# Loading the first weights inside the one block of a two-layer decoder kernel, with head rows picked over 128 rows and a new table of turns

## The chip, the cores and the metric

The kernel runs on one core of one Trainium2 chip. The metric is the device time of one execution in microseconds; lower is better. A time quoted for a kernel is the median of its executions.

## What is computed

The input is x of 8 rows of the batch, 256 positions each, 512 features, and a context of 8 x 256 x 128. Two layers follow, each with a LayerNorm ahead of every part and a residual sum behind it:

```
x = x + attn(ln(x), Wq, bq, Wk, bk, Wv, bv, Wo, bo)   # layer 0: 16 heads, causal
x = x + xattn(ln(x), ctx, ctx)                        # 32 query heads, 8 key heads
x = x + ffn(ln(x), w_gate, w_up, w_down)              # operands rounded to a block format
x = x + ssm(ln(x), Wx, Wg, bg, Wo, A, Dp)             # layer 1: recurrence over 256 steps
x = x + xattn2(ln(x), ctx, Wq, Wkv_expand, Wout)      # 16 heads, causal
x = x + experts(ln(x), W, gate_w, A, B)               # top 2 of 8 low-rank experts
```

The recurrence needs `softplus(delta[h] + B[n])` for 32 heads h and 128 states n. The kernel builds that sum in a bank of PSUM: it adds to the B part the row of `delta` that belongs to head h, spread over all 128 partitions.

## The kernel before

A row is one element of the batch (256 x 512, f32, tile `XR`, five buffers). Each part of a layer is a class (`Attention`, `Mixing`, `Quantised` and `Hidden` for layer 0; `States`, `Attention` again as `cross`, and `Experts` for layer 1). For each engine a part has a generator that yields between steps. `side_by_side` takes a string of letters per engine, the table `TURNS0`; each letter advances one generator by one step. So the order of the instructions on each engine is written out by that table, and the engines meet only at semaphores. All eight rows run through layer 0 and then through layer 1, with neighbouring rows and parts interleaved.

Products of f32 values are made of three f16 products: a weight is split into a high part (a copy by ACT, L271) and a low part (a subtraction by DVE, L277). `Loader` does this for a list of weights, with three staging buffers: the DMA into a staging buffer waits until the low part of the item three places earlier is made.

Ahead of the main block the program has two small blocks.

- In the first (L212) POOL makes the constants `ident`, `ident16`, `identh`, `hide_qk`, `minus_half` and `ones_of_four`.
- In the second (L1774) SP and ACT issue the loads of Wq, Wk, Wv, Wo, bv and of the biases, and ACT and DVE split them. `ffn_room` stages them. A clearing of semaphores with a barrier over all engines follows (`clear`, L180).
- The main block then begins. On POOL it starts with `attn.pool_setup` (L383 to L387: clears `attn_NM` and fills 32 partitions of `attn_stack` twice) and `mix.pool_setup` (L835 to L840 in `mix_V` and `mix_K`), ahead of all turns.

In the main block the first row goes this way. SP loads it (L1802). DVE takes its moments (L323 to L329), POOL the inverse root (L333, L335), ACT scales it (L341), TensorE transposes it (L402), ACT and DVE split the transpose (L555, L607). TensorE multiplies by Wq and Wk (L194 for all such products), ACT and DVE split the result into `attn_P` (L569, L619). SP sends this to `attn_stack` (L694), DVE takes the maxima of the scores (L630, L634) and splits them (L639), and SP sends them on (L700). Then ACT makes the exponentials (L587), POOL masks them (L677), TensorE multiplies by V (L499, L507), and DVE takes the reciprocal of the sums (L643), once per row.

Beside this, `Quantised` rounds the 12 chunks of the ffn weights, 1 MB each: a load into one of two raw buffers in `ffn_room` (L729), and ten DVE steps (L738 to L768), of which four of 128 x 2048 take 2.3 us and two take 1.2 us, and the maximum (L738) 2.3 us.

In layer 1 `States.pe` picks a head's row (L1321): the stationary operand is one column of `pickh` [64, 32], repeated 128 times, the moving operand `ssm_db` [64, 256], in which partitions 0 to 31 hold the high and 32 to 63 the low part of `delta`. There are 256 of these matmuls.

## Time and profile before

| | us |
|---|---|
| median of 3 executions | 1780.51 |
| lowest and highest | 1776.14, 1786.61 |
| the profiled execution | 1775.17 |
| its span, first to last instruction | 1773.4 |
| TensorE, VectorE, ScalarE, GpSimd busy | 1442.2, 1373.2, 1057.3, 429.4 |
| mean granted clock of TensorE | 0.906 of 2.4 GHz |

The profile is that of the one profiled execution. A share of busy time is a mean over stages. PE is TensorE, DVE VectorE, ACT ScalarE, POOL GpSimd, SP the engine that issues most DMAs; SPq is its queue. By the chain that ended last TensorE has 39% of the span, VectorE 29%, ScalarE 16%, issue 9% and GpSimd 3%.

### The profile page before, as it was taken

The page shows a single profiled execution, that of the slowest core. Times are in us where ns is not written, and L with a number is a line of the kernel's source. Part 1 is how long each engine was busy: PE and PEld are TensorE (multiplying, and loading weights), DVE is VectorE, ACT ScalarE, POOL GpSimd, SP SyncE. Part 2 cuts the span into 40 slices and gives each one's busy share as a digit, 9 for nine tenths or more (in the row PEclk, how much of TensorE's full clock was granted, in tenths as well). Part 3 has the DMA queues.
Part 4 walks back from the last instruction along what each step waited for, and adds up shares of the span by engine and source line. Part 5 has one row for each costly group of instructions (what it writes and reads, how often), then busy time and mean ns, then how long its engine had stood idle before and what let it go on. Part 6 is the DMA issues. An engine that isn't in the chain of part 4 may idle for free.

```text
span 1773.4 us, 30964 instructions
## 1 busy us (share of the span) xinstructions
PE 1442.2 (81%) x11863; PEld 725.5 (41%) x11920; DVE 1373.2 (77%) x2111; ACT 1057.3 (60%) x1878; POOL 429.4 (24%) x486
## 2 busy tenths in 40 slices
PE   0767877878988888879878766889998899998986
PEld 0443543344443443444333422345444445454542
DVE  3989998899598796885887897858676877868743
ACT  2242642563743735646566757688869698987531
POOL 4241322151230512311331231212221213030310
PEclk9787978899999999999988987798989899899988
DMA  6302130202002002002210003101010101101010
GB/s 226 87 27 61 55 96 24 67 14 43 26 13 67 13 29 40 26 8 61 76 49 25 25 0 111 40 1 40 25 40 18 47 15 50 37 16 40 13 49 24
DMA packets 92082, 76.38 MB, mean 43 GB/s; under 512 B 9376, under 2 KB 73888, under 8 KB 91424
## 3 DMA queue, kind: packets, MB, share of 16 engines
q1 hardware_dynamic: 91504, 74.14, 15.1%
q8 instruction: 96, 1.57, 0.4%
q14 instruction: 50, 0.41, 0.1%
q10 hardware_dynamic: 432, 0.27, 0.1%
HBM read 39.24 MB, written 9.44 MB: 27 GB/s over the span
## 4 chain that ended last, share of the span: by engine, by line
PE 39%; DVE 29%; ACT 16%; issue 9%; POOL 3%; SPq 1%; DMA 1%; ACTq 0%; DVEq 0%; POOLq 0%
PE bank L194 10%; DVE mix_NM L1025 5%; PE bank L938 3%; PE bank L1125 3%; PE bank L499 3%; PE bank L459 3%; DVE ssm_HS L1485 2%; ACT ssm_DA L1433 2%; PE bank L507 2%; PE bank L487 2%; PE bank L923 2%; DVE ffn_m L1079 2%; PE bank L461 2%; ACT ssm_DD L1436 2%; DVE ffn_Z L1089 1%
## 5 line engine op out<-in xcount | busy, mean ns | idle before, releaser
L998 ACT ACTIVATE mix_P<-bank 128x512 f32<-128x512 f32 x256 | 140.6, 600 | 76.8 <-PE bank L923 75.4
L1485 DVE TENSOR_TENSOR_SCAN ssm_HS<-ssm_DA,ssm_DD 128x1024 f32<-128x1024 f32 x64 | 151.7, 2371 | 31.8 <-ACT ssm_DD L1436 27.2
L1025 DVE TENSOR_REDUCE mix_NM<-bank 128x2 f32<-128x512 f32 x256 | 163.9, 682 | 15.3 <-PE bank L898 14.9
L677 POOL TENSOR_SCALAR_AFFINE_SELECT cross_P<-cross_P 128x256 f32<-128x256 f32 x128 | 90.0, 711 | 331.5 <-ACT cross_P L587 331.4
L677 POOL TENSOR_SCALAR_AFFINE_SELECT attn_P<-attn_P 128x256 f32<-128x256 f32 x128 | 98.6, 782 | 225.1 <-ACT attn_P L587 224.9
L1243 POOL TENSOR_TENSOR ffn_room<-ffn_room 128x512 f32<-128x512 f32 x64 | 87.9, 1373 | 224.0 <-DVE ffn_room L1207 122.9
L1433 ACT ACTIVATE ssm_DA<-ssm_Z,A_T 128x255 f32<-128x255 f32 x256 | 112.6, 503 | 4.5 <-DVE ssm_HS L1485 4.0
L587 ACT ACTIVATE attn_P<-bank 128x384 f32<-128x384 f32 x128 | 63.4, 496 | 66.1 <-PE bank L488 65.7
L587 ACT ACTIVATE cross_P<-bank 128x384 f32<-128x384 f32 x128 | 62.7, 490 | 55.8 <-PE bank L488 55.3
L938 PE MATMUL bank<-mix_P,mix_V 128*32 128x256 f32 x1024 | 74.3, 416 | 11.7 <-DVE mix_XN L1041 11.6
L1125 PE MATMUL bank<-gate,ffn_XQ 128*128 128x512 bf16 x227 | 64.0, 399 | 24.0 <-DVE ffn_room L1207 19.2
L1207 DVE SCALAR_TENSOR_TENSOR ffn_room<-ffn_room,bank 128x512 f32<-128x512 f32 x64 | 43.4, 679 | 50.2 <-ACT ffn_room L1178 50.1
L923 PE MATMUL bank<-mix_Q,mix_K 64*128 64x256 f16 x512 | 53.2, 286 | 35.4 <-ACT mix_P L998 19.3
L1491 DVE TENSOR_TENSOR ssm_HS<-ssm_HS,ssm_CS 128x1024 f32<-128x1024 f32 x64 | 78.7, 1230 | 1.0
L1408 ACT ACTIVATE ssm_Z<-bank 128x512 f32<-128x512 f32 x128 | 71.6, 596 | 10.2 <-PE bank L1321 9.6
L898 PE MATMUL bank<-mix_K,mix_Q 64*128 64x256 f16 x512 | 53.1, 286 | 28.3 <-DVE mix_NM L1025 24.7
L1125 PE MATMUL bank<-up,ffn_XQ 128*128 128x512 bf16 x247 | 70.5, 410 | 1.7 <-issue 1.0
L1436 ACT ACTIVATE ssm_DD<-ssm_Z 128x1024 f32<-128x1024 f32 x64 | 67.6, 1056 | 0.0
L1178 ACT ACTIVATE ffn_room<-bank 128x512 f32<-128x512 f32 x64 | 38.2, 598 | 46.0 <-PE bank L1125 45.9
L1151 PE MATMUL bank<-down,ffn_room 128*128 128x512 bf16 x237 | 61.9, 393 | 1.6 <-issue 0.8
L487 PE MATMUL bank<-attn_stack 128*128 128x256 f16 x128 | 39.2, 306 | 27.6 <-ACT attn_P L587 21.3
L1321 PE MATMUL bank<-ssm_db,pickh 64*128 64x256 f16 x256 | 49.4, 296 | 14.7 <-ACT ssm_Z L1408 13.7
(403 smaller groups left out, 4141.3 us busy)
## 6 DMA issues: line engine op xcount, KB each, us to landing
attn_stack<-attn_P SPq DMA_DIRECT2D x64, 128.0 KB, 2.5
cross_stack<-cross_P SPq DMA_DIRECT2D x64, 128.0 KB, 2.5
XR<-x SPq DMA_DIRECT2D x8, 512.0 KB, 4.6
ffn_room<-f_gate SPq DMA_DIRECT2D x4, 1024.0 KB, 7.7
attn_stack<-attn_P SPq DMA_DIRECT2D x64, 64.0 KB, 2.1
ffn_room<-f_up SPq DMA_DIRECT2D x4, 1024.0 KB, 5.2
ffn_room<-f_down SPq DMA_DIRECT2D x4, 1024.0 KB, 4.9
x_mid<-XR SPq DMA_DIRECT2D x8, 512.0 KB, 3.0
```

Source lines behind the costliest of these rows:

```text
L194: last = nc.tensor.matmul(out, a_, b_, start=(start and i == 0), stop=(stop and i == len(terms) - 1))
L587: nc.scalar.activation(self.p[h % 8][:, :], bank[self.b[0]][:, 0:S + P], ACT.Exp, scale=HD1 ** -0.5).then_inc(self.p_ready, 1)
L677: nc.gpsimd.affine_select(out=diagonal, in_=diagonal, compare_op=ALU.is_ge, fill=0.0, base=0, pattern=[[0, 2], [1, P]], channel_multiplier ...
L923: last = nc.tensor.matmul(bank[b4[i]][:, k * S:(k + 1) * S], self.k[rows, v // 2, k * P:(k + 1) * P], self.q[rows, v, :], start=(k == 0), ...
L938: last = nc.tensor.matmul(bank[b][32 * j:32 * j + 32, half * S:(half + 1) * S], self.v[:, k, g, :], self.p[(4 * g + j) % 8][:, k * S:(k + ...
L998: nc.scalar.activation(self.p[h % 8], bank[b4[h % 2]][:, :], ACT.Exp, scale=HD2 ** -0.5).then_inc(s["p_ready"], 1)
L1025: nc.vector.tensor_reduce(self.nm[:, t, 16 * i + 2 * g:16 * i + 2 * g + 2], bank[b4[u % 3]][:, :].rearrange("p (c k) -> p c k", c=2), AX.X ...
L1125: last = nc.tensor.matmul(bank[b][:, :], self.xq[:, k, T * P:(T + 1) * P], w[:, k, fb * 512:(fb + 1) * 512], start=(k == 0), stop=(k == DC ...
L1243: nc.gpsimd.tensor_tensor(self.inter[q % 2][:, 512 * (g % 2):512 * (g % 2) + 512], self.sg[g % 2], self.up[g % 2], ALU.mult).then_inc(s["i ...
L1433: nc.scalar.activation(self.da[:, G % 2, k, 1:S], self.z[:, h, 1:S], ACT.Exp, scale=self.A_T[:, h:h + 1])
L1436: nc.scalar.activation(self.dd[:, G % 2, :, :], self.z[:, HG * g:HG * g + HG, :], ACT.Square).then_inc(s["da_ready"], 1)
L1485: nc.vector.tensor_tensor_scan(flat(self.hs), flat(self.da), flat(self.dd), 0.0, ALU.mult, ALU.add).then_inc(s["hs_ready"], 1)
```

## The change

The two small blocks are gone. What they did is now in the main block.

- SP gets two more streams, the weights and the biases. Their staging is now `attn_stack` (two halves) and the front of `attn_P`, no longer `ffn_room`. bv comes ahead of Wo.
- ACT and DVE get one more stream each, for the splitting.
- POOL makes the constants first. `attn.pool_setup` and `mix.pool_setup` become streams with turns of their own; the first waits until all five weights are split.
- TensorE waits for the constants once, for the low parts of Wq and Wk ahead of the first product, for the fourth item (bv) ahead of the first V, for all ahead of the first product with Wo. ACT waits for all five and for the biases ahead of its first split of q and k (which writes where Wv was staged), and SP ahead of the first DMAs into `attn_stack`. POOL waits for the biases ahead of adding bo.
- Loaders that share semaphores count on from the items before (`first`, `used`), since nothing is cleared between them.
- `pickh` and `ssm_db` are 128 partitions high; partitions 64 to 127 of `ssm_db` are set to 0 once, on POOL, in place of a second writing of one column. The pick is a matmul over 128 rows.
- The table of turns is another one for all engines.

```diff
             def sp(self, sp, i, free=None):
...
                 if i >= n:
-                    sp.wait_ge(self.low_ready, i - n + 1)
+                    sp.wait_ge(self.low_ready, self.first + i - n + 1)
...
-                        if n == B:
-                            pe.wait_ge(weights_f.low_ready, len(weights_f.items))
+                        if n == self.first:
+                            pe.wait_ge(*self.weights.ready(2))
...
+                    if n == self.first and t == 0 and self.bv is not None:
+                        pe.wait_ge(*self.weights.ready(4))
...
-                    if n == B and c == 0:
-                        act.wait_ge(weights_f.low_ready, len(weights_f.items))
+                    if n == self.first and c == 0:
+                        act.wait_ge(*self.weights.ready())
+                        if self.bq is not None:
+                            act.wait_ge(small_in, 48)
...
-                        last = nc.tensor.matmul(bank[b][:, i * S:(i + 1) * S], self.pickh[:, 2 * u + i:2 * u + i + 1].broadcast_to([2 * NH, P]),
+                        last = nc.tensor.matmul(bank[b][:, i * S:(i + 1) * S], self.pickh[:, 2 * u + i:2 * u + i + 1].broadcast_to([P, P]),
...
-            weights_0 = Loader("l0w", [(whole(w), chunk(A[n])) for w, n in ((wq, "Wq"), (wk, "Wk"), (wv, "Wv"), (wo, "Wo"))]
-                               + [(whole(bv), A["bv"].partition_broadcast(P))],
-                               [room[:, 2048 * i:2048 * i + 2048] for i in range(3)])
+            weights_0 = Loader("l0w", [(whole(w), chunk(A[n])) for w, n in ((wq, "Wq"), (wk, "Wk"), (wv, "Wv"))]
+                               + [(whole(bv), A["bv"].partition_broadcast(P)), (whole(wo), chunk(A["Wo"]))],
+                               [attn.stack[:, i, :, :].rearrange("p h k -> p (h k)").bitcast(F32) for i in range(2)]
+                               + [attn.space[:, 0:2048]])
...
-            pickh = sb(l1, "pickh", [2 * NH, NH], F16)
+            pickh = sb(l1, "pickh", [P, NH], F16)
...
-            db = sb(l1, "ssm_db", [2 * NH, S], F16)
+            db = sb(l1, "ssm_db", [P, S], F16)
...
-        clear([r.num for r in weights_0.loaded + [weights_0.high_ready, weights_0.low_ready, small_in, done_pool]])
...
+        def clear_attention(pool, n):
+            yield
+            pool.wait_ge(*weights_0.ready())
+            attn.pool_setup(pool)
+
+        def clear_mixing(pool, n):
+            yield
+            mix.pool_setup(pool)
...
+                             in_turn(lambda i: weights_0.sp(sp, i), items_0),
+                             in_turn(lambda n: load_biases(sp, n), 1),
...
                 own = Own(pool, done_pool)
-                attn.pool_setup(pool)
-                mix.pool_setup(pool)
-                side_by_side(TURNS0["pool"], in_turn(lambda n: attn.norm.pool(pool, own, n)),
+                make_constants(own)
+                side_by_side(TURNS0["pool"], in_turn(lambda n: clear_attention(pool, n), 1),
+                             in_turn(lambda n: clear_mixing(pool, n), 1),
+                             in_turn(lambda n: attn.norm.pool(pool, own, n)),
```

A line or two of the table of turns, SP's:

```diff
-        "caaaaaeeccbebeeebbcceeebbcceeccbebccbccbdaccbccdabccdabccccbdccbccbdcckkkffjkkkccdfcdfllldgflllg"
+        "eacleaaakkkackkebcbeeebbeebccbeeccebccbeccbccbdaccbdaccbccdabccbccdccbccbdccjmmfmfmmmccdfcdfnnnd"
```

How the instructions of three queues stand now. First SP, from the start of the main block of the changed kernel (`f_gate` are chunks of the ffn weights, `ctx_cols` and `ctx_rows` the context, `a_...` the weights and biases of the first attention, `x` the rows):

```order
L739 DMA ffn_room<-f_gate 128x4x512
L1804 DMA XR<-x 128x2x512
L857 DMA mix_CF<-ctx_cols 128x256
L861 DMA mix_VR<-ctx_rows 128x128 x2
L1789 DMA l_bq<-a_bq 128x4
L1789 DMA l_bk<-a_bk 128x4
L1789 DMA l_bo<-a_bo 128x512
L739 DMA ffn_room<-f_gate 128x4x512
L1804 DMA XR<-x 128x2x512 x3
L266 DMA attn_stack<-a_Wq 128x4x512
L266 DMA attn_stack<-a_Wk 128x4x512
L266 DMA attn_P<-a_Wv 128x4x512
```

Before, SP had the four weights and bv in a block of their own, and then the context, five rows and two chunks; now a chunk, row 0, the context, the biases, the second chunk and rows 1 to 3 stand ahead of Wq.

DVE before, in the main block behind its first instruction (L738 to L750 are the rounding of chunk 0, L607 the low part of the transposed first row):

```order
L323 BN_STATS attn_stats<-XR 128x6 x2
L326 BN_AGGR attn_mv<-attn_stats 128x2 x2
L328 TENSOR_SCALAR attn_negative<-attn_mv 128x2
L329 TENSOR_SCALAR attn_var<-attn_mv 128x2
L738 TENSOR_REDUCE w_max<-ffn_room 128x64
L607 TENSOR_TENSOR attn_XL<-bank,attn_XH 128x4x128 x2
L323 BN_STATS attn_stats<-XR 128x6 x2
L326 BN_AGGR attn_mv<-attn_stats 128x2 x2
L328 TENSOR_SCALAR attn_negative<-attn_mv 128x2
```

DVE of the changed kernel, from the maximum of chunk 0 on (L278 makes a low part, L615 is the former L607, L748 to L778 the former L738 to L768):

```order
L748 TENSOR_REDUCE w_max<-ffn_room 128x64
L751 TENSOR_SCALAR w_max<-w_max 128x64
L753 TENSOR_SCALAR w_e<-w_max 128x64
L755 TENSOR_SCALAR w_inv<-w_e 128x64
L757 TENSOR_SCALAR w_sc<-w_e 128x64
L760 TENSOR_TENSOR ffn_room<-ffn_room,w_inv 128x2048
L278 TENSOR_TENSOR l_wq_l<-attn_stack,l_wq_h 128x2048
L278 TENSOR_TENSOR l_wk_l<-attn_stack,l_wk_h 128x2048
L278 TENSOR_TENSOR l_wv_l<-attn_P,l_wv_h 128x2048
```

and, after the low parts of Wk, Wv and bv and the moments of row 1:

```order
L330 TENSOR_SCALAR attn_var<-attn_mv 128x2
L615 TENSOR_TENSOR attn_XL<-bank,attn_XH 128x4x128 x2
L763 TENSOR_SCALAR ffn_room<-ffn_room 128x2048
L766 TENSOR_SCALAR ffn_room<-ffn_room 128x2048
L769 SCALAR_TENSOR_TENSOR ffn_room<-ffn_room 128x2048
L278 TENSOR_TENSOR l_wo_l<-attn_stack,l_wo_h 128x2048
L772 TENSOR_TENSOR ffn_room<-ffn_room 128x2048
L627 SCALAR_TENSOR_TENSOR attn_P<-bank,l_bq,attn_P 128x256
```

Before, all five low parts stood in front of everything, and only the chunk's maximum stood ahead of the low part of the transposed row. Now five steps of chunk 0 and four low parts do, and the low part of Wo stands behind three more steps of the chunk and ahead of the first split of q (L627).

POOL before, at the start of the main block (`attn_NM` and `attn_stack` are cleared and filled by `attn.pool_setup`, `mix_V` and `mix_K` by `mix.pool_setup`):

```order
L383 MEMSET attn_NM 128x64
L385 MEMSET attn_stack 32x4096
L387 MEMSET attn_stack 32x4096
L835 MEMSET mix_V 128x512
L838 MEMSET mix_K 32x2048 x2
L840 MEMSET mix_V 128x16
L1050 MEMSET mix_P 128x64x16
L333 ISA
L333 TENSOR_TENSOR attn_rstd<-attn_var,minus_half 128x2
L335 TENSOR_TENSOR attn_shift<-attn_negative,attn_rstd 128x2
L671 TENSOR_TENSOR XR<-XR,l_bo 128x1024
```

POOL of the changed kernel, after the constants:

```order
L1060 MEMSET mix_P 128x64x16
L334 TENSOR_TENSOR attn_rstd<-attn_var,minus_half 128x2
L336 TENSOR_TENSOR attn_shift<-attn_negative,attn_rstd 128x2
L681 TENSOR_TENSOR XR<-XR,l_bo 128x1024
L334 TENSOR_TENSOR attn_rstd<-attn_var,minus_half 128x2
L336 TENSOR_TENSOR attn_shift<-attn_negative,attn_rstd 128x2
L385 MEMSET attn_NM 128x64
L387 MEMSET attn_stack 32x4096
L389 MEMSET attn_stack 32x4096
L845 MEMSET mix_V 128x512
L848 MEMSET mix_K 32x2048 x2
L850 MEMSET mix_V 128x16
```

Before, `attn_NM`, both fills of `attn_stack`, `mix_V` and `mix_K` stood ahead of the first inverse root; now only the clearing of `mix_P` does, and they stand behind the roots of rows 0 and 1; the first mask (L687) follows them.

## Rows read from the trace of the kernel before

**Rows 1.** The page: busy time, and 40 slices of the span (tenths)

```profile
PE 1442.2 (81%) x11863; PEld 725.5 (41%) x11920; DVE 1373.2 (77%) x2111; ACT 1057.3 (60%) x1878; POOL 429.4 (24%) x486
...
DVE  3989998899598796885887897858676877868743
...
PEclk9787978899999999999988987798989899899988
```

**Rows 2.** Windows: length; PE, PEld, DVE, ACT, POOL busy (count); clock, DMA share, GB/s

```profile
0.00:25.00 25.00, 0.00 (x0) 0.00 (x0) 9.77 (x5) 9.49 (x6) 2.36 (x19) 1.00 0.56 189
25.00:50.00 25.00, 9.01 (x58) 7.25 (x59) 12.34 (x24) 3.94 (x7) 18.32 (x13) 1.00 0.64 221
```

**Rows 3.** Timeline of the opening: start, duration, engine, line, operation, idle before

```profile
3.58 0.43 SPq L265 DMA_DIRECT2D ffn_room<-a_Wq  x1
...
9.80 1.90 ACT L271 CAST l_wq_h<-ffn_room 128x2048 f16<-128x2048 f32 x1 [3.35 <-DMA ffn_room<-a_Wq]
11.73 2.29 DVE L277 TENSOR_TENSOR l_wq_l<-ffn_room,l_wq_h 128x2048 f16<-128x2048 f32 x1 [11.73 <-ACT l_wq_h L271]
...
23.36 0.69 DVE L277 TENSOR_TENSOR l_bv_l<-ffn_room,l_bv_h 128x512 f16<-128x512 f32 x1
25.02 0.34 SPq L847 DMA_DIRECT2D mix_CF<-ctx_cols  x1
...
25.23 3.51 POOL L385 MEMSET attn_stack<- 32x4096 f16 x1
...
26.35 2.48 SPq L1802 DMA_DIRECT2D XR<-x  x5
...
32.95 3.65 POOL L838 MEMSET mix_K<- 32x2048 f16 x2
...
37.70 0.71 POOL L333 TENSOR_TENSOR attn_rstd<-attn_var,minus_half 128x2 f32<-128x2 f32 x1
...
38.72 1.52 ACT L341 ACTIVATE attn_XN<-XR,attn_shift,attn_rstd 128x512 f32<-128x512 f32 x2 [11.26 <-POOL attn_shift L335]
39.05 2.29 DVE L738 TENSOR_REDUCE w_max<-ffn_room 128x64 f32<-128x2048 f32 x1 [6.71 <-DMA ffn_room<-f_gate]
...
42.21 0.69 DVE L607 TENSOR_TENSOR attn_XL<-bank,attn_XH 128x512 f16<-128x512 f32 x1 [0.16 <-ACT attn_XH L555]
...
42.96 0.40 PE L194 MATMUL bank<-attn_XH,l_wq_h 128*128 128x256 f16 x1 [1.40 <-DVE attn_XL L607]
```

**Rows 4.** Timeline of the first row's attention, DVE

```profile
48.34 0.48 DVE L619 SCALAR_TENSOR_TENSOR attn_P<-bank,l_bq,attn_P 128x256 f16<-128x256 f32 x1 [0.81 <-ACT attn_P L569]
...
49.13 1.22 DVE L753 TENSOR_SCALAR ffn_room<-ffn_room 128x2048 int32<-128x2048 int32 x1
...
57.49 0.47 DVE L619 SCALAR_TENSOR_TENSOR attn_P<-bank,l_bq,attn_P 128x256 f16<-128x256 f32 x1
...
103.66 1.76 DVE L643 RECIPROCAL attn_RC<-bank 128x256 f32<-128x256 f32 x1 [3.76 <-PE bank L507]
```

**Rows 5.** The same timeline, ACT: the first exponential

```profile
79.61 0.49 ACT L587 ACTIVATE attn_P<-bank 128x384 f32<-128x384 f32 x1 [3.68 <-PE bank L488]
```

**Rows 6.** Windows in which the DMA engines are full

```profile
9.80:16.50 6.70, 0.00 (x0) 0.00 (x0) 3.01 (x2) 3.79 (x2) 0.00 (x0) 1.00 0.98 339
28.00:41.00 13.00, 1.41 (x7) 1.42 (x8) 4.04 (x7) 1.78 (x3) 10.96 (x10) 1.00 1.01 363
```

**Rows 7.** Line L1321, the picks: duration ns min/median/max, first and last start

```profile
L1321 PE MATMUL bank<-ssm_db,pickh x256: 267/269/418, 929.6 to 1638.1; 64*128 64x256 f16 x128
```

**Rows 8.** The page's group for the picks: busy, mean ns, idle before, releaser

```profile
L1321 PE MATMUL bank<-ssm_db,pickh 64*128 64x256 f16 x256 | 49.4, 296 | 14.7 <-ACT ssm_Z L1408 13.7
```

**Rows 9.** Window of low clock in the second half, all engines

```profile
1301.00:1305.00 4.00, 4.00 (x15) 1.01 (x13) 3.33 (x5) 0.00 (x0) 0.00 (x0) 0.50 0.69 149
```

**Rows 10.** TensorE groups by shape in that window

```profile
L459 PE MATMUL bank<-cross_P 32*128 32x256 f16 x10 | 3.0, 402 | 0.0
```

**Rows 11.** Line L643 in the second half: one reciprocal closes each row's attention

```profile
L643 DVE RECIPROCAL cross_RC<-bank x8: 1756/1758/1759, 1179.6 to 1728.9; 128x256 f32<-128x256 f32 x8
```

More of the change, by code:

```diff
@@ L247, in __init__, with ready @@
                     self.loaded, self.high_ready, self.low_ready = before.loaded, before.high_ready, before.low_ready
+                self.first = 0 if before is None else len(before.items)
+                self.used = [0 if before is None else len(range(i, len(before.items), len(stage))) for i in range(len(stage))]
+            def ready(self, count=None):
+                return self.low_ready, self.first + (len(self.items) if count is None else count)
             def staged(self, i):
@@ L357, in __init__ @@
                 self.qk = self.space[:, 0:2 * DC * S].bitcast(F16).rearrange("p (i c k) -> p i c k", i=4, c=DC)
-                self.rest = 3 if before is None else 6
+                self.rest, self.first = (3, 0) if before is None else (6, B)
+                self.weights = weights
                 for_sems = lambda part: sem(f"{name}_{part}") if before is None else before.signals[part]
@@ L534, in pe @@
                         b = self.b[(2 + t) % 3]
+                        if n == self.first and c == 0 and t == 0 and self.bv is not None:
+                            pe.wait_ge(*self.weights.ready())
                         if c == 0:
@@ L682, in sp @@
                 sp.wait_ge(self.qk_ready, DC * n + DC)
-                if n == B:
-                    sp.wait_ge(weights_f.low_ready, len(weights_f.items))
+                if n == self.first:
+                    sp.wait_ge(*self.weights.ready())
                 if n:
```

212 lines of the change are left out of this document (101 added, 111 removed).

## The prediction

> **What bounds the kernel now.** I read the page first. TensorE is busy for 81% of the span and VectorE for 77%, so neither is full everywhere; the slices show DVE at 9 tenths from the third slice on, and low only in the first two [rows 1]. So the opening is the place to look, and I went on to windows. In the first 25 us DVE works 9.77 us, ACT 9.49 and TensorE not at all; in the next 25 TensorE works 9.01 and DVE 12.34 [rows 2]. DVE is thus idle for 27.9 of the first 50 us, in a stretch behind which it is the busiest engine.
>
> The timeline of the opening gives the chain [rows 3]. The first weight is asked for at 3.58, behind the block of constants, and lands by 9.80. The last low part (bv) starts at 23.36 and ends at 24.05; the first DMA of the main block is issued at 25.02. Then POOL clears: `attn_stack` from 25.23, 3.51 us and as long again, `mix_K` until 36.60. Its first inverse root comes only at 37.70, and ACT, which scales row 0 at 38.72, had been idle for 11.26 us for it. DVE waits 6.71 us for chunk 0 and has its maximum at 39.05. The low part of row 0 starts last at 42.21, and the first product with Wq at 42.96. From there DVE leads: its first split of q starts at 48.34, the last at 57.49 [rows 4], the first exponential at 79.61 [rows 5], the reciprocal at 103.66 [rows 4].
>
> **The change part by part.** *Start of the DMAs.* SP has no work in the block of constants, so its first issue moves from 3.58 to about 0.8, where POOL's first constant is written in this trace (an estimate). The barrier, the clearing of semaphores and the second start go too, 0.97 us from 24.05 to 25.02 [rows 3].
>
> *Landing of the weights.* They now queue behind other bytes: two chunks (2.10 MB), rows 0 to 3 (2.10), context (0.26), bo (0.26). Wq, Wk and Wv add 1.05 MB each. With the DMA engines full they moved 363 GB/s over 13 us, and 339 among the weights alone [rows 6]. I take 363, since the mixture of chunks and rows is that of that window. The first weight took 2 us before bytes flowed, so they flow from 2.8. Wq has 5.77 MB up to its end: 18.7. Wk lands at 21.6, Wv at 24.5. With 339 Wv lands at 26.0. The Trainium skill (DMA: Bandwidth & Descriptors, section "Where 436 GB/s comes from") puts the limit of HBM for one core at about 358 GB/s; by it Wv would land at 24.8, and the trace's 363 stands just above it.
>
> *Split of the weights.* ACT needs 1.90 us and DVE 2.29 us for one of 128 x 2048 [rows 3]. While waiting, DVE does row 0's moments, the maximum of chunk 0 and its first multiplication, 2.29 each; all that is over by about 16.5. Low parts then end at 18.7 + 1.90 + 2.29 = 22.9 (Wq), 25.8 (Wk), 28.7 (Wv), 29.4 (bv, 0.69). The moments of row 1 take 1.8 (1.29 at L323 and three short ones), the two low parts of the transposed row 1.4. So the first product with Wq starts at **32.6**, against 42.96: 10.4 us sooner, and chunk 0 is one multiplication further.
>
> *First split of q.* ACT may write where Wv was staged only after all five splits. Wo is issued once Wk is split (25.8), lands at about 30 behind row 4 and bv, and is cast by 32. DVE comes to it after three steps of the chunk (1.22, 1.23 and 2.28, the durations of [rows 4]): 32.6 + 4.7 + 2.3 = 39.6. ACT then needs 0.94, DVE one more long step (41.9), and the four pairs of L627 with one long step between end at about 48, against 58.4. That is again 10.4, and DVE has then done the whole of chunk 0, one long step more than before.
>
> *The rest of row 0's attention.* The steps are the same and DVE has the same rounding to do up to the reciprocal (three chunks in both). SP's 16 DMAs to `attn_stack` follow the split of q, and the six for `mix_K`, formerly early, stand behind them, ahead of the maxima; they end before the maxima are split, so they cost nothing while DVE is behind. POOL's clearing, 7.2 us and 4.3 for the mixing, starts behind the low part of Wo, 39.6, and `attn_stack` is done at 46.8; DVE's first maximum that waits for it comes at about 54. It is covered by 7 us; if that cover went, its excess would be added to the first exponential. I put the first exponential at 69 and the reciprocal at 93, **10.7 us** sooner: the 10.4, and 0.3 of the long step by which DVE is further on.
>
> *What is added.* The same five splits stay, 9.85 us of DVE, now beside transfers. The clearing of 64 partitions of `ssm_db` is one memset on POOL, in place of another: nothing, under the cover of POOL's 24% load.
>
> *Picks over 128 rows.* 256 picks, 267 ns at the least, 418 at the most, median 269, mean 296 [rows 7, 8]: about 46 ran at the low clock, (296-269)/(418-269) of 256. If none did, that gives 46 x 0.149 = 6.9 us of TensorE at most. The lower bound is 0: the idle time before picks is 14.7 us, 13.7 of it for ACT [rows 8], so TensorE is not what leads there. That it could help at all, rows show: from 1301 to 1305 TensorE is busy for 4.00 of 4.00 us and the granted clock is 0.50, that is 1.2 GHz [rows 9], and most of that time goes to matmuls of 32 rows [rows 10]. I take 1.3, near the lower bound, since ACT leads. The Trainium skill (TensorE: Matmul & The Clock Gate, section "What's actually happening") says that the level follows how busy TensorE has been; wider picks keep it as busy as before, so by that rule this term is 0 and the forecast 1.3 us later. The window of [rows 9] speaks against the rule taken alone.
>
> *The table.* 1976 turns of TensorE before and now, and the rows of each part stand nearly where they stood. No row prices it. The nearest rows are the gaps: the 7 passes of the second half take (1728.9-1179.6)/7 = 78.5 us each [rows 11], with TensorE and DVE both at 6 to 9 tenths [rows 1], so room for gain and loss in each. I take 0, with 0.5 us per pass in 14 passes either way: -7 to +7.
>
> Sum: -10.7 - 1.3 + 0 = **-12.0 us**. The profiled execution (1775.17, span 1773.4) would become 1763.2. The median shown, 1780.5, is 5.3 above it; what is asked is a median, so the forecast is 1780.5 - 12.0 = **1768.5**.
>
> **The rivals.**
> *A. The weights come late.* Everything that SP puts ahead of Wq delays it. Should the mixture run at about 290 GB/s, between the 339 of the weights [rows 6] and the 221 of the second 25 us [rows 2], Wv lands at 29.9, the first product is at 38, and 5.4 of the 10.4 us are gone: -6.6, 1773.9. For it: the ramp in the first slices. Against: the full window of 13 us [rows 6].
> *B. The gain is swallowed.* DVE, 9 tenths busy up to slice 10 [rows 1], carries the opening's gain only if its order has no new wait; one wait for a maximum or a bank of 1.5 us in each of 7 passes of layer 0 uses it up: 1780.
> *C. Slower: the new order stalls each pass of the second half.* There ACT, DVE and TensorE feed one another through three banks. Should a pick or a scan come one step late in each of the 7 passes and once in the handover, 3 us each, that is 24 us: 1780.5 - 12 + 24 = 1792.5. It decides from 1.5 us per pass on. Against it: the parts stand at nearly the same turns.
> *D. The table gains too.* The same mechanism with the other sign, 1.5 us in each of 7 passes: 1758.
>
> **How the numbers follow.** Forecast 0.50, A 0.15, B 0.12, C 0.08, D 0.15. What a measurement of this kernel can tell from no change is 0.5%, 8.9 us: faster means under 1771.6, slower over 1789.4. Faster: D, and 0.45 of the forecast's 0.50 (the table at +4 or more takes the rest), and 0.03 of A: 0.63. Slower: 0.07 of C. Same: 0.30. The range: below, 1768.5 less 5.6 for picks, less 7 for the table: 1756; above, plus 1.3, 3.2 of the 5.4 of A and 7: 1780. It holds the forecast, A, most of D and half of B.
>
> **What the changed profile should show.** SP's first DMA by 1.3 us; Wv landed at 24 to 26; the first product with Wq at 31 to 35; the low part of Wo by 40; `attn_stack` filled by 47 and no wait of DVE for it; first exponential at 68 to 71; first reciprocal at 92 to 95; the last reciprocal of `cross_RC` at about 1717. Picks with a mean under 296 ns would show the clock's part. I am wrong if the reciprocal of row 0 is at 93 and the later ones are not 10 us sooner (B, C), or if it is later than 97 (A).

## The result and the profile after

| | before | after |
|---|---|---|
| median of 4 executions each, us | 1778.33 | 1712.43 |
| lowest and highest | 1773.25, 1786.61 | 1709.06, 1717.3 |
| span of the profiled execution | 1773.4 | 1707.2 |
| mean granted clock | 0.906 | 0.918 |

The ratio is 0.9627, with a 95% interval of 0.9582 to 0.9672: 66 us faster, where 12 were forecast, and far below the range of 1756 to 1780. Two executions ran far slower at a far lower clock (1981.83 us at 0.67 for the kernel before, 2046.15 at 0.639 for wide_alone below), and no ratio of this document counts them.

The page of the changed kernel, busy time and slices, against [rows 1]:

```profile
PE 1407.3 (82%) x11862; PEld 726.6 (43%) x11920; DVE 1372.5 (80%) x2111; ACT 1034.3 (61%) x1862; POOL 434.4 (25%) x486
...
DVE  6979989998689796895878799977697878877743
...
PEclk9888889799999998998999989879999998998998
```

VectorE has the same work (1372.5 us against 1373.2) in a shorter span. Its idle time went from 1773.4 - 1373.2 = 400.2 to 1707.2 - 1372.5 = 334.7: 65.5 us, nearly all of the 66.2 between these two spans. TensorE also lost 34.9 us of busy time with the same number of matmuls, and its clock is higher (0.918 is the highest of the four executions of the changed kernel, 0.910 the lowest).

The windows of the opening, with the columns of [rows 2]:

```profile
0.00:25.00 25.00, 1.94 (x8) 1.57 (x8) 11.63 (x14) 7.59 (x8) 6.61 (x23) 1.00 0.95 320
25.00:50.00 25.00, 16.14 (x113) 12.10 (x114) 23.72 (x26) 8.22 (x13) 9.89 (x7) 1.00 0.24 82
```

VectorE is busy for 35.35 of the first 50 us, before for 22.11. So 13.2 of the 65.5 us of idle time are won there. To split the rest I cut both traces where VectorE first takes the moments of a layer 1 row (883 us before, 865 after). The last parts of layer 0 still run beyond that cut; where "layer 1" is said of a window, it is the time from the cut on. Its windows, before and then after:

```profile
883.00:1773.00 890.00, 752.67 (x5836) 374.80 (x5850) 656.21 (x1026) 626.15 (x1110) 187.84 (x213) 0.89 0.12 33
```

```profile
865.00:1707.00 842.00, 712.56 (x5800) 373.60 (x5806) 653.22 (x1027) 600.47 (x1087) 194.68 (x213) 0.93 0.13 36
```

VectorE's idle time there is 890.0 - 656.2 = 233.8 before and 842.0 - 653.2 = 188.8 after: **45 us**. Layer 0 behind the opening has the other 7. So by these two traces two thirds of the gain lie in a half of the program that the forecast gave nothing but its 1.3 us for picks.

VectorE's waits over the whole span, before and after (what it waits for, us in total, times, longest):

```profile
DVE ffn_room L1207 <- ACT ffn_room L1178: 50.1, 21, 6.2
DVE ssm_HS L1485 <- ACT ssm_DD L1436: 27.2, 19, 4.5
DVE ssm_ML L1516 <- ACT ssm_MH L1449: 20.3, 11, 3.2
...
DVE attn_NM L630 <- PE bank L454: 12.5, 4, 7.0
...
DVE attn_NM L634 <- PE bank L461: 9.2, 18, 3.2
```

```profile
DVE ffn_room L1217 <- ACT ffn_room L1188: 33.0, 19, 7.7
...
DVE attn_NM L642 <- PE bank L465: 19.7, 20, 10.2
...
DVE ssm_HS L1495 <- ACT ssm_DD L1446: 14.7, 11, 4.3
...
DVE ssm_ML L1526 <- ACT ssm_MH L1459: 10.7, 7, 3.0
...
DVE attn_NM L638 <- PE bank L458: 1.1, 2, 0.7
```

Three waits for ScalarE shrink by 17.1, 12.5 and 9.6 us. Those of the first attention's maxima for TensorE stay as they were in sum, 12.5 + 9.2 before and 19.7 + 1.1 now. What went is no single wait but several of one kind. All of VectorE's waits added up by the engine waited for make it plainer (each row is one trace; the runs are those of the next section):

| kernel | turns | picks | waits for ScalarE, us | waits for TensorE, us |
|---|---|---|---|---|
| before | old | 64 | 194.9 | 164.5 |
| wide_alone | old | 128 | 191.3 | 168.7 |
| open_alone | old | 64 | 186.3 | 175.4 |
| front_new | old behind row 0 | 128 | 187.1 | 166.1 |
| table_alone | new | 64 | 153.1 | 167.6 |
| pick64 | new | 64 | 142.2 | 168.5 |
| changed | new | 128 | 135.4 | 160.6 |

The new turns take some 40 us out of the waits for ScalarE and nothing out of those for TensorE. In table_alone VectorE's whole idle time falls by 40.3 us (to 1732.2 - 1372.3 = 359.9), and its waits for ScalarE by 41.8. The wide picks take 4 to 9 us out of the waits for TensorE in layer 1 (pick64 97.9, changed 88.9; open_alone 92.8, front_new 85.6; before 89.7, wide_alone 86.0).

The timeline of the opening, against [rows 3] and [rows 4]:

```profile
0.79 0.43 SPq L739 DMA_DIRECT2D ffn_room<-f_gate  x1
...
8.49 3.28 SPq L266 DMA_DIRECT2D attn_stack<-a_Wk  x1
...
11.82 2.37 SPq L266 DMA_DIRECT2D attn_P<-a_Wv  x1
...
20.62 1.90 ACT L272 CAST l_wq_h<-attn_stack 128x2048 f16<-128x2048 f32 x1 [7.11 <-DMA attn_stack<-a_Wq]
...
22.55 2.29 DVE L278 TENSOR_TENSOR l_wq_l<-attn_stack,l_wq_h 128x2048 f16<-128x2048 f32 x1 [4.32 <-ACT l_wq_h L272]
...
26.03 1.90 ACT L272 CAST l_wv_h<-attn_P 128x2048 f16<-128x2048 f32 x1 [0.75 <-DMA attn_P<-a_Wv]
...
27.96 2.29 DVE L278 TENSOR_TENSOR l_wv_l<-attn_P,l_wv_h 128x2048 f16<-128x2048 f32 x1 [0.35 <-ACT l_wv_h L272]
...
33.86 0.39 PE L194 MATMUL bank<-attn_XH,l_wq_h 128*128 128x256 f16 x1 [18.97 <-DVE attn_XL L615]
...
38.44 2.28 DVE L278 TENSOR_TENSOR l_wo_l<-attn_stack,l_wo_h 128x2048 f16<-128x2048 f32 x1
...
44.56 3.51 POOL L389 MEMSET attn_stack<- 32x4096 f16 x1
```

```profile
69.63 0.49 ACT L595 ACTIVATE attn_P<-bank 128x384 f32<-128x384 f32 x1 [3.68 <-PE bank L492]
...
96.08 1.76 DVE L651 RECIPROCAL attn_RC<-bank 128x256 f32<-128x256 f32 x1 [7.46 <-PE bank L511]
```

The MEMSET at 44.56 is the second filling of `attn_stack`; it ends at 48.1. SP starts at 0.79. The first product with Wq is at 33.86 (42.96 before), the first exponential at 69.63 (79.61), the reciprocal of row 0 at 96.08 (103.66).

### The profile page after: what moved, and what is told of

It reads as the page before. It is cut to its first block, busy times and chain, and to the rows that moved or that the text cites. A ratio compares the mean times of both kernels' runs of the same rounds, so it can differ in the third digit from the quotient of the medians.

```text
span 1707.2 us, 30917 instructions
## 1 busy us (share of the span) xinstructions
PE 1407.3 (82%) x11862; PEld 726.6 (43%) x11920; DVE 1372.5 (80%) x2111; ACT 1034.3 (61%) x1862; POOL 434.4 (25%) x486
## 4 chain that ended last, share of the span: by engine, by line
DVE 34%; PE 33%; ACT 12%; issue 9%; SPq 5%; POOL 3%; DMA 2%; ACTq 0%; DVEq 0%; POOLq 0%
PE bank L194 10%; DVE mix_NM L1035 6%; DVE ssm_HS L1495 4%; PE bank L1135 3%; SPq L704 3%; PE bank L503 2%; PE bank L948 2%; DVE ffn_m L1089 2%; POOL attn_P L687 2%; DVE ffn_Z L1099 2%; PE bank L511 2%; PE bank L491 2%; PE bank L933 2%; ACT ssm_DA L1443 2%; PE bank L463 1%
## 5 line engine op out<-in xcount | busy, mean ns | idle before, releaser
L687 POOL TENSOR_SCALAR_AFFINE_SELECT cross_P<-cross_P 128x256 f32<-128x256 f32 x128 | 95.3, 754 | 301.8 <-ACT cross_P L595 301.7
L1495 DVE TENSOR_TENSOR_SCAN ssm_HS<-ssm_DA,ssm_DD 128x1024 f32<-128x1024 f32 x64 | 151.1, 2361 | 20.5 <-ACT ssm_DD L1446 14.7
L687 POOL TENSOR_SCALAR_AFFINE_SELECT attn_P<-attn_P 128x256 f32<-128x256 f32 x128 | 99.9, 791 | 248.1 <-ACT attn_P L595 247.8
L1418 ACT ACTIVATE ssm_Z<-bank 128x512 f32<-128x512 f32 x128 | 72.2, 601 | 19.7 <-PE bank L1331 19.2
L948 PE MATMUL bank<-mix_P,mix_V 128*32 128x256 f32 x1024 | 70.4, 396 | 3.8 <-DVE mix_XN L1051 3.0
L1331 PE MATMUL bank<-ssm_db,pickh 128*128 128x256 f16 x256 | 49.4, 297 | 11.3 <-ACT ssm_Z L1418 10.3
L642 DVE TENSOR_REDUCE attn_NM<-bank 128x2 f32<-128x512 f32 x64 | 42.0, 685 | 20.1 <-PE bank L465 19.7
```

What stands on the lines that cost most here:

```text
L687: nc.gpsimd.affine_select(out=diagonal, in_=diagonal, compare_op=ALU.is_ge, fill=0.0, base=0, pattern=[[0, 2], [1, P]], channel_multiplier ...
L948: last = nc.tensor.matmul(bank[b][32 * j:32 * j + 32, half * S:(half + 1) * S], self.v[:, k, g, :], self.p[(4 * g + j) % 8][:, k * S:(k + ...
L1495: nc.vector.tensor_tensor_scan(flat(self.hs), flat(self.da), flat(self.dd), 0.0, ALU.mult, ALU.add).then_inc(s["hs_ready"], 1)
```

## The experiments

In the runs below a "cut" joins two tables: the turns of one up to a named step of VectorE and all that this step waits for, on each engine, and the turns of the other, in their order, behind it. Each ratio is to the kernel before, with its 95% interval, and 1779 us turn a ratio into a time.

| run | opening | picks | turns | ratio | interval |
|---|---|---|---|---|---|
| open_alone | new | 64 | old, new to row 0's reciprocal | 0.9943 | 0.9918-0.9967 |
| wide_alone | old | 128 | old | 0.9925 | 0.99-0.995 |
| table_alone | old | 64 | new | 0.9715 | 0.9685-0.9745 |
| pick64 | new | 64 | new | 0.9696 | 0.9673-0.9719 |
| pick96 | new | 96 | new | 0.9634 | 0.9604-0.9663 |
| front_new | new | 128 | new to row 0's reciprocal | 0.9928 | 0.99-0.9955 |
| two_rows_new | new | 128 | new to row 1's reciprocal | 0.998 | 0.996-0.9999 |
| l0_new | new | 128 | new through layer 0 | 0.9828 | 0.9795-0.9861 |
| to_cross2_new | new | 128 | new to the second cross row | 0.9661 | 0.9626-0.9696 |
| to_cross4_new | new | 128 | new to the fourth cross row | 0.9707 | 0.968-0.9733 |
| l1_new | old | 64 | new in layer 1 alone | 0.984 | 0.9807-0.9874 |
| hand_only | old | 64 | new in the handover alone | 0.991 | 0.9878-0.9942 |

**Picks over 64 rows again** (pick64).

```diff
-    self.pickh[:, 2 * u + i:2 * u + i + 1].broadcast_to([P, P])
+    self.pickh[:, 2 * u + i:2 * u + i + 1].broadcast_to([2 * NH, P])
-    pickh = sb(l1, "pickh", [P, NH], F16)
+    pickh = sb(l1, "pickh", [2 * NH, NH], F16)
-    db = sb(l1, "ssm_db", [P, S], F16)
+    db = sb(l1, "ssm_db", [2 * NH, S], F16)
...
-    nc.gpsimd.memset(db[2 * NH:P, :], 0.0).then_inc(made, 1)
+    nc.gpsimd.memset(one_column[:, NH - 1:NH], 1.0).then_inc(made, 1)
```

> The changed kernel with its picks over 64 rows again (pickh, ssm_db 64 partitions high), all else as changed. Theory T (the new order of turns carries most of the 66 us): 1712 to 1718, ratio to the kernel before about 0.963 to 0.967. Theory W (the wider matmuls hold TensorE's clock up in layer 1, and that is most of the 33 us that layer 1 gained between its first and last row): 1735 or more, ratio 0.975 or higher, and a granted clock in 1000 to 1400 us back at 0.82 to 0.90.

It took 1723.65 us, ratio 0.9696, between the two theories: the wide picks are worth 0.0069, about 12 us (3 to 21 by the two intervals), and the other 54 lie elsewhere.

**New turns to row 0's reciprocal, then the old ones** (front_new), through all of layer 0 (l0_new), and in layer 1 alone in the program before (l1_new). One line of each table's difference stands for all, here TensorE's in front_new, turns 66 to 95:

```diff
-aaaaaaaaabbaaaaaaaaaaaaacaaaaa
+aaaaaaabbabbabaaaabaababababab
```

> The changed program (one block, wide picks), with the new turns only up to the reciprocal of row 0 in layer 0 and what that needs, and the order of the kernel before from there on. It prices the opening and the wide picks without the new order. Theory T: the opening's 7.6 us at that reciprocal are carried to the end and little else: 1768 to 1772, ratio 0.994 to 0.997. Theory W: 25 us and more below before, ratio under 0.986. A third (O): the opening's gain is lost in the old order and only a new order could use it: ratio 0.998 to 1.002.

> The changed program, with the new turns up to the first row's moments in layer 1 and what they need, and the old order from there. Theory T: the lead over before at that place, 18 to 25 us in the trace, is kept and not more: 1753 to 1762, ratio 0.986 to 0.991. Theory W: 45 us or more below before, ratio 0.975 or less, since the picks are wide.

> The kernel before (two small blocks, picks over 64 rows), with its own turns up to the first row's moments in layer 1 and the new turns from there. Theory T: layer 1 gives its 35 to 48 us by order alone: 1730 to 1743, ratio 0.973 to 0.980. Theory W: under 15 us, ratio 0.992 or higher.

front_new gave 0.9928, a little more gain than its theory T. l0_new gave 0.9828 and l1_new 0.984, each between the ranges of its two theories. The new turns of layer 0 are thus worth some 18 us behind the new opening (1.00% of 1779, by the two intervals 8 either way), and those of layer 1 alone 28 us (22 to 34). The idle time of the one pair of traces put only 7 us into layer 0; a single trace is uncertain by as much (last section).

**Each part alone.** table_alone is the program before with the new letters, those of the new streams struck out. wide_alone is the program before with

```diff
-                nc.scalar.copy(self.db[:, :], bank[zb[1]][0:2 * NH, 0:S])
+                nc.scalar.copy(self.db[0:2 * NH, :], bank[zb[1]][0:2 * NH, 0:S])
-            nc.gpsimd.memset(one_column[:, NH - 1:NH], 1.0).then_inc(made, 1)
+            nc.gpsimd.memset(db[2 * NH:P, :], 0.0).then_inc(made, 1)
+            pool.wait_ge(made, at + 1)
```

beside the widths. open_alone is front_new with pick64's edit. pick96 has `[96, P]` in place of `[P, P]`, and tiles of 96 partitions.

> The kernel before with its two small blocks and its picks over 64 rows, and the whole new order of turns (less the turns of the streams that do not exist there). If order, opening and picks add up: the picks over 64 rows with all else new were 53 us below before and the opening is worth about 8, so 43 to 47 us here, ratio 0.974 to 0.977. Rival: the new order was made for a program that starts earlier and loses part of its worth without it: ratio 0.982 or higher.

> The kernel before with its picks over 128 rows, nothing else. Front_new (new opening, wide picks, old order) was 14 us below before, of which the opening's reciprocal shows 8: so 5 to 7 us here, ratio 0.996 to 0.997. Rival: the wide picks are worth the same 12 us as beside the new order, ratio 0.993 or less. Second rival: nothing, 0.999 to 1.001.

> The changed program's opening (one block, new turns up to the first reciprocal), picks over 64 rows, old order from there. The opening's lead at the first reciprocal, 8 us, is carried to the end: ratio 0.995 to 0.996. Rival: half of it is lost behind in the old order, ratio 0.998 or higher.

> The changed kernel with picks over 96 rows, 32 of zeros in place of 64. If it is the number of rows that a matmul spans, by degrees, that keeps TensorE's clock up: between the two, 1714 to 1721, ratio 0.964 to 0.968, and cold time in layer 1 between 128 and 173 us. If there is a step between 64 and 128, it lies at one of the two: 1712 (0.963) or 1724 (0.970). If width has nothing to do with it and the 12 us are the chance of one layout: anything, with no order among the three.

The **table** alone gives 0.9715, **51 us** less (45 to 56). The **picks** alone give 0.9925, **13 us** (9 to 18). The **opening** gives 0.9943, **10 us** (6 to 15). The product of the three is 0.9587, and 0.9627 was measured: 7 us short of the plain product, which the intervals are wide enough to explain. 96 rows do as well as 128 within the intervals. Of the expectations, the table alone gave more than either of its theories, the opening a little more than its first, and wide_alone met its rival: the 5 to 7 us expected had been taken as the difference of two other numbers. pick96 leaves open whether the effect comes by degrees or in a step: its ratio is that of 128 rows, its time at the low clock (below) lies between.

The order in which the parts are added matters, as far as the intervals tell. With the new table first, the steps are 51 us for the table, 3 for the opening behind it (0.9715 to 0.9696, some 7 either way) and 12 for the picks. In the old order, behind the new opening, the picks give 3 us (open_alone 0.9943 to front_new 0.9928, some 7 either way), where before them they gave 13. So three pairs of kernels that differ in the width of the picks alone show 12, 13 and 3 us. Why the third is smaller was not settled.

What the wide picks do is in the clock. The mean granted clock of all executions behind the ratios shows it, lowest and highest of each kernel:

| all else as in | 64 rows | 96 rows | 128 rows |
|---|---|---|---|
| before | 0.890 to 0.907 (20 executions) | | wide_alone, 0.908 to 0.918 (8) |
| changed | pick64, 0.904 to 0.908 (4) | pick96, 0.908 to 0.915 (6) | changed, 0.910 to 0.918 (4) |
| front_new | open_alone, 0.895 to 0.905 (12) | | front_new, 0.902 to 0.914 (9) |

The new table raises the clock too: table_alone has 0.905 to 0.914 (6 executions). So part of its 51 us may be the clock; the sums of waits above put nearly all of the idle time that it saves to waits for ScalarE.

Windows of layer 1 in pick64 (to compare with the one of the changed kernel above), and in wide_alone (to compare with the one of before above):

```profile
865.00:1722.00 857.00, 735.90 (x5792) 371.35 (x5798) 653.05 (x1025) 601.47 (x1086) 189.32 (x213) 0.90 0.13 35
```

```profile
892.00:1771.00 879.00, 730.99 (x5842) 378.30 (x5854) 653.84 (x1029) 624.67 (x1111) 191.25 (x214) 0.91 0.12 34
```

With the same turns and the same instructions but for that width, TensorE's busy time in layer 1 falls from 735.90 to 712.56 us (23.3), and the granted clock rises from 0.90 to 0.93. In the old order it falls from 752.67 to 730.99, and the clock rises from 0.89 to 0.91. By the clock's records the time at 1.2 GHz in layer 1 is 173 us with 64 rows, 157 with 96 and 128 with 128 (196 and 159 in the old order). The picks themselves hardly gain. Their group in the page, pick64 and then the changed kernel:

```profile
L1331 PE MATMUL bank<-ssm_db,pickh 64*128 64x256 f16 x256 | 50.7, 305 | 10.9 <-ACT ssm_Z L1418 10.2
```

```profile
L1331 PE MATMUL bank<-ssm_db,pickh 128*128 128x256 f16 x256 | 49.4, 297 | 11.3 <-ACT ssm_Z L1418 10.3
```

50.7 against 49.4 us: 1.3. The other 22 us of busy time are in the matmuls around them. The largest single one I can show is that of 32 rows in the second attention, in layer 1 (line, shape, count, busy, mean ns), pick64 and then the changed kernel:

```profile
L463 PE MATMUL bank<-cross_P 32*128 32x256 f16 x128 | 31.5, 335 | 1.2 <-DVE cross_NM L638 1.2
```

```profile
L463 PE MATMUL bank<-cross_P 32*128 32x256 f16 x128 | 28.2, 305 | 1.5 <-DVE cross_NM L638 1.2 <-DVE cross_NM L642 0.4
```

**Where in the table.** The two traces show VectorE's reciprocals of layer 0 ahead by 7.6, 24.4, 29.0, 23.4, 6.3, 22.9, 25.4 and 16.4 us, row by row, so the lead at row 1 looked like a gain of 17 us in one pass. In layer 1 the lead grew from 34 to 56 us over the third pass. two_rows_new, to_cross2_new and to_cross4_new cut there.

> The changed kernel (one block, 128-row picks), its own turns up to the reciprocal of the second head row of layer 0 (the reciprocal group named attn_RC with row number 1), the order before after it. The new order stands about 24 us ahead of the old at that reciprocal, of which the opening is about 8. Theory 1 (a lead won in layer 0 is lost again by the handover to layer 1, because the old order's waits there swallow it): the same as the run with the new turns to the first reciprocal only (ratio 0.9928), so 0.990 to 0.994. Theory 2 (every pass's lead is kept): 16 us less than that run, 0.982 to 0.986, as the run with all of layer 0 new (0.9828).

> The changed kernel with its own turns through layer 0 and until the second row's moments of layer 1, the order before after them. Theory 1 (the gain in layer 1 is made at two places, the handover to it and the third pass): this holds the handover's part alone, some 5 to 8 us under the run with layer 0 new (0.9828), so 0.978 to 0.980. Theory 2 (layer 1 gains evenly in every pass): 36 us of layer 1 over eight rows, two rows are 9 us, 0.977 to 0.979; what tells the theories apart is the next run.

> The changed kernel with its own turns through layer 0 and until the fourth row's moments of layer 1, the order before after them. Theory 1 (third pass of layer 1 and the handover hold nearly all of its gain, since the lead at the reciprocals of that layer goes from 34 to 56 us over the third pass and only to 66 by the end): 0.966 to 0.970. Theory 2 (evenly by pass): half of the 36 us are left out, 0.972 to 0.975.

two_rows_new is slower than front_new by 9 us, which neither theory had. VectorE's waits behind its cut, from 165 to 285 us:

```profile
DVE attn_XN L657 <- PE bank L526: 13.5, 2, 13.3
DVE mix_NM L1035 <- PE bank L908: 4.7, 10, 1.8
```

One wait of 13.3 us for a product (L526) is the seam (the reciprocal of the third row is at 284.9, in front_new at 271.4): the new turns had put VectorE's part of row 1 first, and the old ones ask for what TensorE had put off. So a run cut inside a pass measures its seam too, and this one says nothing on row 1 but that its early reciprocal is no time in hand. Being ahead at one step is not being ahead in work.

to_cross2_new gave 0.9661 where both theories had 0.977 to 0.980. The step from l0_new is 30 us (0.9828 to 0.9661, some 9 either way), so the handover and the first two rows of layer 1 hold nearly all that layer 1 gains here. What is left to the changed kernel, 0.9661 to 0.9627, lies inside the intervals. (l1_new and hand_only, in the old program, read otherwise: 0.984 against 0.991 leaves 12 us, some 8 either way, to the turns behind the handover.) The third pass was a false trail. Its window in the changed kernel, and in to_cross2_new:

```profile
1215.00:1291.00 76.00, 70.52 (x622) 39.54 (x621) 60.63 (x101) 67.55 (x120) 19.11 (x23) 0.98 0.15 38
```

```profile
1197.00:1289.00 92.00, 80.60 (x674) 44.86 (x666) 70.24 (x108) 78.52 (x138) 20.11 (x23) 0.96 0.12 31
```

The changed kernel takes 76 us for that pass, to_cross2_new 92, and yet they stand level behind it (reciprocal at 1290.8 and 1289.3): VectorE does 70.24 us of work in to_cross2_new and 60.63 in the changed kernel. Of the 16 us between them 9.6 are work that had been moved over the mark and 6.4 are idle time; to_cross2_new had been 18 us ahead at the mark, and both end within 3.5 us of each other (last reciprocals below). to_cross4_new, with more new turns, is not better (0.9707), which fits a seam again but was not settled. It lies between its two theories, and its interval (0.968 to 0.9733) reaches into both, so it decides nothing.

**The handover alone** (hand_only). The program before; of VectorE's 1356 turns 111 read otherwise, between numbers 712 and 942, and of TensorE's 1976 turns 167, between 993 and 1327. SP's part of the edit:

```diff
-bdcckkkffjkkkccdfcdfllldgflllghhhghifg
+bdcckkkfjfkkkccdfcdfllldgflllhghhghifg
```

> The kernel before (two blocks, 64-row picks), its own order everywhere but from the first layer-1 row's moments to the second cross row's, where the new turns stand: of TensorE 167 of 1976 turns read otherwise, of VectorE 111 of 1356, of ScalarE 176 of 1540. Theory 1 (the table's gain sits at the handover from layer 0 to layer 1): 20 to 28 us less than before, ratio 0.984 to 0.989, nearly what the new turns in all of layer 1 gave (0.984); the way from the third row's moments of ssm to the fourth's shortens from 119 to some 90 us. Theory 2 (the new order pays only as a whole, since each piece prepares the next): at most 10 us, 0.994 or more.

It gave 0.991: 16 us (10 to 22), between the two theories. The reciprocals of the second attention, first and last start behind the colon, in hand_only, to_cross2_new and the changed kernel:

```profile
L643 DVE RECIPROCAL cross_RC<-bank x8: 1756/1757/1758, 1173.3 to 1720.4; 128x256 f32<-128x256 f32 x8
```

```profile
L651 DVE RECIPROCAL cross_RC<-bank x8: 1757/1758/1759, 1134.3 to 1666.1; 128x256 f32<-128x256 f32 x8
```

```profile
L651 DVE RECIPROCAL cross_RC<-bank x8: 1752/1758/1759, 1146.6 to 1662.6; 128x256 f32<-128x256 f32 x8
```

Of before they start at 1179.6 and end with 1728.9 [rows 11]. hand_only is ahead by 6.3 at the first, 12.4 at the second and 8.5 at the last, though its layer 0, with the old turns, ended 4 us later in this trace. So the old turns carry most of the lead made in the handover through six more passes. Here is the lead made. Windows of before: from layer 1's first moments to the second row's reciprocal, and two stretches within it:

```profile
883.00:1249.00 366.00, 288.72 (x2103) 135.13 (x2118) 290.16 (x417) 255.68 (x445) 86.11 (x81) 0.86 0.12 36
...
1034.00:1073.00 39.00, 24.51 (x112) 8.70 (x116) 38.04 (x47) 16.91 (x29) 10.37 (x6) 0.78 0.00 1
1073.00:1093.00 20.00, 14.84 (x72) 5.56 (x70) 13.04 (x13) 15.60 (x19) 0.00 (x0) 0.83 0.61 214
```

and the same of hand_only:

```profile
887.00:1237.00 350.00, 278.78 (x2109) 133.39 (x2125) 287.36 (x419) 253.22 (x446) 90.09 (x82) 0.89 0.13 38
...
1040.00:1070.00 30.00, 20.10 (x110) 7.77 (x112) 29.41 (x35) 18.33 (x30) 5.98 (x4) 0.83 0.00 1
1070.00:1100.00 30.00, 21.79 (x121) 9.35 (x122) 27.96 (x25) 29.74 (x46) 1.93 (x1) 0.88 0.49 162
```

The stretch shrinks from 366 to 350 us with VectorE's work nearly unchanged (290.16, 287.36), so its idle time falls from 75.8 to 62.6. Before, VectorE alternates scans of the recurrence (L1485) with rounding of the last ffn from 1034 to 1073, while ScalarE is busy for only 16.91 of 39 us. Then VectorE lacks work: 13.04 of 20 us are busy from 1073 on. Its timeline there:

```profile
1083.76 0.69 DVE L1516 SCALAR_TENSOR_TENSOR ssm_ML<-bank,ssm_MH 128x512 f16<-128x512 f32 x1 [2.41 <-ACT ssm_MH L1449]
1086.35 0.69 DVE L1516 SCALAR_TENSOR_TENSOR ssm_ML<-bank,ssm_MH 128x512 f16<-128x512 f32 x1 [1.90 <-ACT ssm_MH L1449]
1088.63 2.29 DVE L277 TENSOR_TENSOR xq_w_l<-cross_stack,xq_w_h 128x2048 f16<-128x2048 f32 x1 [1.58 <-ACT xq_w_h L271]
...
1100.32 0.69 DVE L277 TENSOR_TENSOR f_b_l<-cross_P,f_b_h 128x512 f16<-128x512 f32 x1 [3.36 <-ACT f_b_h L271]
```

Each of these waits is for ScalarE: for `ssm_MH`, and for the high parts of weights, which ScalarE makes only when its own turns have come round. What is missing there are the scans: before has one at 1073.37 and the next only at 1104.35. In hand_only the roundings stand nearly where they stood (1036 to 1072), but fewer scans are among them, and the scans left over stand beside the splits of the weights:

```profile
1074.04 2.28 DVE L1485 TENSOR_TENSOR_SCAN ssm_HS<-ssm_DA,ssm_DD 128x1024 f32<-128x1024 f32 x1
...
1079.52 2.28 DVE L1485 TENSOR_TENSOR_SCAN ssm_HS<-ssm_DA,ssm_DD 128x1024 f32<-128x1024 f32 x1
...
1086.07 2.29 DVE L1485 TENSOR_TENSOR_SCAN ssm_HS<-ssm_DA,ssm_DD 128x1024 f32<-128x1024 f32 x1 [0.60 <-ACT ssm_DD L1436]
```

From 1070 to 1100 VectorE has 27.96 of 30 us and ScalarE 29.74. Over the 89 us around it VectorE's idle time is 3.8 us (1011 to 1100), in before 10.1 (1009 to 1098): the 6.3 us of lead at the first reciprocal.

## Why the prediction was wrong

**The table: 0 with a bound of 7 forecast, 51 us measured.** This is the step that failed. It argued that "the rows of each part stand nearly where they stood" and bounded the term by 0.5 us in each of 14 passes. Neither follows from a row. The count of turns and the place of a part say nothing on who waits for whom. The prediction's first reading, which made the opening the only place to look, is wrong too: it has VectorE's slices low only in the first two, but these are 3 and 9, and behind the tenth they fall to 5 three times and stay mostly at 6 to 8 from the 26th on [rows 1]. What the trace did offer was VectorE's idle time, 400 us of 1773.4 in the page [rows 1], of which only 27.9 are in the opening. An order can win from all of it. The new table alone takes 40.3 us of it, 30.6 of them in layer 1 (table_alone: 858.0 - 654.8 = 203.2, before 233.8), and nearly all of that from waits for ScalarE. Rival D had the mechanism but was built on the same small step, 1.5 us in 7 passes. It gave 1758, 46 us too high. Nor does the gain come pass by pass, as D and C had it. Some 18 us come with layer 0's turns, and 16 with the handover alone in the old program. Behind the new layer 0 the handover and first two rows give 30, and the passes after it next to nothing that these runs can tell; in the old program those passes give 12, some 8 either way.

**Picks: -1.3 forecast, -12, -13 and -3 measured.** This term failed as well, though less certainly. The bounds were 0 and 6.9; the interval of wide_alone (9 to 18) lies outside them, those of the two pairs (3 to 21, and 4 more to 9 less) do not. The sum counted the picks' own time at the low clock. They did save 1.3 us of their own against pick64, which equals the forecast by chance, since that had been taken against before, where their time is the same 49.4 us. The named sign, a mean under 296 ns, did not come (297). But the higher clock then held for matmuls that nobody had changed, 22 us of busy time in layer 1, of which about half reached the end. That TensorE is not what leads at the picks was read from their waits for ScalarE [rows 8], and remains true of them. But the gain is made elsewhere. The Trainium skill (TensorE: Matmul & The Clock Gate, section "What's actually happening") has the level follow how busy TensorE has been. The trace does not bear that out taken alone. In layer 1 TensorE was busy for 735.90 of 857 us (86%) at a clock of 0.90, and for 712.56 of 842 (85%) at 0.93; these are means over half the program, and a low clock itself makes matmuls last longer. The stretch around [rows 9] says more:

```profile
1297.00:1309.00 12.00, 12.00 (x46) 3.68 (x46) 9.12 (x11) 3.56 (x7) 0.00 (x0) 0.50 0.50 110
```

TensorE of before was busy for 12.00 of 12.00 us and was granted 0.50 throughout, that is 1.2 GHz. The 16 matmuls of 32 rows (L459) are the largest group there, 4.8 us. [rows 9] had pointed the right way and was given too little weight.

**The opening: -10.7 forecast, -10 measured in the old order, -3 behind the new table.** The first (6 to 15) agrees better than the parts do, so its closeness is partly luck; the second has 7 us either way. At the reciprocal of row 0 the lead was 7.6. By parts: SP's first DMA at 0.79 (0.8). Wq is cast at 20.62, where 18.7 was forecast, and Wv at 26.03 (24.5). The rate was not the main error:

```profile
2.80:26.00 23.20, 1.94 (x8) 1.57 (x8) 12.31 (x15) 6.59 (x7) 4.55 (x6) 1.00 1.03 352
```

From 2.8 us, where the forecast let bytes flow, to 26.0 the transfers moved 352 GB/s, not the 363 of [rows 6]. But by 26.0 that is 8.4 MB, where the forecast had 7.87 up to the end of Wv: the 0.5 MB more is the size of row 4, which SP issued at 14.23, while Wv was under way. SP's own issues of Wk and Wv took 3.28 and 2.37 us, which no term had; that they delayed the landing is not shown. The last low part ahead of the first product (bv) ends at 30.9, 1.5 later than forecast. The first product is at 33.86 (32.6), 9.1 us sooner instead of 10.4. Rival A thus took 1.3 of the 5.4 us that it threatened. The low part of Wo ended at 40.72 (39.6), `attn_stack` was filled by 48.1 (46.8), still ahead of the maxima, and the exponential started at 69.63 (69). Here the forecast lost 3 us: VectorE waits 7.46 us for TensorE ahead of the reciprocal, at 96.08 instead of 93. In the old order front_new is ahead by 8.6 to 8.8 us from the third row to the sixth and 5.3 at the eighth, open_alone by 8.3 to 8.5 from the fourth to the sixth, 5.1 at the eighth and 4.4 at the end; pick64 is ahead of table_alone by 9.8 to 13.3 at every row to the end. Single traces differ by as much, so it is the ratio of open_alone (at most 0.9967) that speaks against rival B, which had all of it lost.

**Rival C** (3 us of new waits per pass of the second half) did not come as a sum: a pass there takes (1662.6 - 1146.6)/7 = 73.7 us, before 78.5. VectorE's scans wait 14.7 us for ScalarE instead of 27.2, and the picks wait 10.3 us for it instead of 13.7. One wait of its kind did grow: ScalarE now waits 19.2 us for the picks, before 9.6.

The named signs told it plainly: the last reciprocal was to be at about 1717 and is at 1662.6.

## What to carry to other kernels

Do not put zero on a new order because its parts stand at nearly the same turns: take the idle time of the busiest engine, part by part of the program, as what an order can win, and let that set the range. When two orders are compared, a lead at one marked step is worth only what the work done by then says; count busy time up to the mark, and look for a seam before believing a cut table. A gain that two changes share shows only when one is measured with and without the other: here the opening is worth 10 us in the old order and 3 behind the new table, some 7 either way. Where a matmul's shape changes in a stretch that runs partly at the low clock, price the clock for all of TensorE's work in that stretch, not for the matmuls touched.

## What the runs showed of the hardware

- Rows of zeros raised TensorE's clock, by all executions of three pairs of kernels (0.890 to 0.907 against 0.908 to 0.918, 0.904 to 0.908 against 0.910 to 0.918, and 0.895 to 0.905 against 0.902 to 0.914). The same 256 picks, with the same columns and nearly the same shortest duration (267 ns with 64 rows [rows 7], 271 with 128), took the time at 1.2 GHz in layer 1 from 173 us to 157 with 96 rows and to 128 with 128 rows (one trace each; for their worth see the next point). The kernel became 12 us faster. Which property of a wider matmul counts was not separated. The width changes more than the rows of zeros: ahead of the picks TensorE's weight loading stood idle, for no cause that the profile shows, for 19.6 to 23.7 us in all in the six traces with 64 rows that were looked at, and for 4.2 to 6.0 in the four with 96 or 128.
- The same layer 0, with the same turns, took 883 us in the trace of before, 887 in that of hand_only, 889 in that of l1_new and 892 in that of wide_alone, and had 140, 157, 157 and 167 us at the low clock. Differences of less than 10 us between single traces, or of less than some 30 us of time at the low clock, are therefore no evidence; for them the ratios and the clocks over all executions count.
- It stays open why the handover's turns are worth 16 us in the old program and, with the two rows behind it, 30 behind the new layer 0. The trace of to_cross2_new has 123 us at the low clock in layer 1 where l0_new has 170, and their mean clocks over four executions each are 0.912 to 0.924 and 0.906 to 0.910, so part of it may be the clock, but no run took the two apart.
